# A transformer block on one core: query and key scratch doubled by parity, and the first layer norm's normal form made by GpSimd

## What is computed

```python
mod = (silu(c) @ wmod).reshape(16, 6, 1, 128)          # sa, ca, ga, sb, cb, gb per batch
h = layernorm(x) * (1 + ca) + sa                        # LN1
q, k, v = h @ wq.T + bq, h @ wk.T + bk, h @ wv.T + bv   # 16 heads of 8
scores = q @ k.T * 8 ** -0.5 + band                     # a key counts only within 32 tokens
x = x + ga * (softmax(scores) @ v @ wo.T + bo)
h = layernorm(x) * (1 + cb) + sb                        # LN2
top2 = top_k(softmax(h @ gate_w.T), 2)                  # 8 experts, 2 for each token
ffn = sum over the chosen e of (silu(s_e*h @ w1[e]) * (s_e*h @ w3[e])) @ w2[e]   # s_e: the score
x = x + gb * (ffn + the shared expert's silu(h @ w1s) * (h @ w3s) @ w2s)
```

## Time and profile before

| | us |
|---|---|
| median of three runs | 745.36 |
| the profiled execution | 746.85 |
| its span in the trace | 745.1 |

### The profile page before, as it was taken

How to read it: one execution, slowest core, us unless ns; L and a number is a source line. 1 busy time by engine, 2 the same in 40 slices (tenths; PEclk the granted TensorE clock), 3 DMA queues, 4 the chain that set the end, 5 groups by cost and what they waited for, 6 DMA issues and landing times.

```text
span 745.1 us, 18977 instructions
## 1 busy us (share of the span) xinstructions
PE 660.5 (89%) x5934; PEld 558.9 (75%) x5934; DVE 581.2 (78%) x1541; ACT 613.0 (82%) x2602; POOL 541.2 (73%) x564
## 2 busy tenths in 40 slices
PE   2267798999989999999899999989899989979886
PEld 1155677878878887878788887878788878878765
DVE  5446667988969898989889898969798888867553
ACT  4276779998979999999999899979899998875442
POOL 4430418887868989788878888868968886758784
PEclk9996557999989999999999999999999999999999
DMA  4747586777676777777677878577777676713120
GB/s 147 181 97 189 131 203 183 187 214 192 181 184 186 200 205 199 190 213 184 175 187 213 204 195 214 163 197 200 189 187 204 161 201 174 188 41 136 64 83 14
DMA packets 193860, 127.70 MB, mean 171 GB/s; under 512 B 110640, under 2 KB 170848, under 8 KB 193632
## 3 DMA queue, kind: packets, MB, share of 16 engines
q1 hardware_dynamic: 193760, 126.50, 64.3%
HBM read 96.29 MB, written 30.17 MB: 170 GB/s over the span
## 4 chain that ended last, share of the span: by engine, by line
PE 42%; DMA 22%; SPq 13%; POOL 8%; issue 6%; ACT 5%; DVE 3%; POOLq 0%; DVEq 0%; ACTq 0%
DMA k<-k_scr 15%; PE ps_s L1209 11%; PE ps_Y L1277 10%; SPq L315 8%; DMA r_scr<-rst 6%; PE ps_O L1232 5%; ACT p L675 4%; SPq L323 3%; PE ps_A L1152 3%; POOL xl L495 3%; POOL xs L489 2%; PE ps_M L1260 2%; PE ps_A L1153 2%; PE ps_A L1154 2%; PE ps_B L1152 2%
## 5 line engine op out<-in xcount | busy, mean ns | idle before, releaser
L675 ACT ACTIVATE p<-ps_s,nmx 128x96 f32<-128x96 f32 x1024 | 332.3, 345 | 58.4 <-DVE nmx L878 57.8
L675 ACT ACTIVATION_READ_ACCUMULATOR p<-ps_s,nmx 128x1 f32 x1024 | 215.7, 211 | 0.0
L1209 PE MATMUL ps_s<-k,q 128*128 128x96 f32 x1024 | 167.2, 297 | 54.1 <-DMA k<-k_scr 42.2
L1209 PEld LDWEIGHTS ps_s<-k,q 128*128 128x128 f32 x1024 | 147.6, 210 | 81.4 <-DMA k<-k_scr 50.2
L878 DVE TENSOR_REDUCE nmx<-ps_s 128x4 f32<-128x384 f32 x256 | 138.0, 548 | 67.4 <-PE ps_s L1209 64.0
L495 POOL TENSOR_TENSOR xl<-xs,xh 128x512 fp32r<-128x512 f32 x128 | 163.4, 1282 | 20.7 <-ACT xh L697 20.7
L489 POOL TENSOR_TENSOR xs<-h,sbc 128x512 f32<-128x512 f32 x128 | 164.0, 1287 | 4.1 <-DMA sbc<-s_scr 4.1
L1277 PE MATMUL ps_Y<-w2s,g 128*128 128x128 f32 x1152 | 163.4, 290 | 0.6 <-DVE g L984 0.6
L1277 PEld LDWEIGHTS ps_Y<-w2s,g 128*128 128x128 f32 x1152 | 150.2, 202 | 4.7 <-DVE g L984 0.8
L895 DVE STREAM_TRANSPOSE pt<-p 128x384 f32<-128x384 f32 x256 | 136.1, 558 | 6.1 <-PE ps_O L1232 4.4
L975 DVE SCALAR_TENSOR_TENSOR th<-th,ps_A 128x512 f32<-128x512 f32 x144 | 97.7, 678 | 36.2 <-ACT th L718 36.1
(11 more groups left out here) (119 smaller groups left out, 920.4 us busy)
## 6 DMA issues: line engine op xcount, KB each, us to landing
sbc<-s_scr SPq DMA_DIRECT2D x64, 512.0 KB, 5.6
k<-k_scr SPq DMA_DIRECT2D x64, 384.0 KB
q<-q_scr SPq DMA_DIRECT2D x128, 96.0 KB
k<-k_scr SPq DMA_DIRECT2D x32, 336.0 KB
q_scr<-qh SPq DMA_DIRECT2D x32, 256.0 KB, 2.5
k_scr<-kh SPq DMA_DIRECT2D x32, 256.0 KB, 2.6
xt<-x SPq DMA_DIRECT2D x16, 256.0 KB, 6.0
q_scr<-ql SPq DMA_DIRECT2D x16, 256.0 KB, 2.5
```

Source lines behind the costliest of these rows:

```text
L675: last = nc.scalar.activation(p[:, n % PRING, gg, :], ps_s[:, n % 2, MK * gg:MK * gg + MK], ACT.Exp, bias=nmx[:, n, gg:gg + 1], accum_out= ...
L1209: last = mm(ps_s[:, n % 2, MK * gg:MK * gg + MK], heads[:, h, gg, nl], k4[:, h, gg, :, MB * nl:MB * nl + MB], start=gg == 0, stop=gg == HG ...
```

## The change

Three things change.

- `q_scr` and `k_scr` get a leading dimension of 2. Batch b writes and reads the copy `b % 2`. The wait in `put_q(b)` on the loads becomes one on the loads of batch b-2, which are those of the same copy.
- The normal form of LN1 (`l1_xn`) is written by POOL, with four `tensor_scalar` instructions that multiply by the token's scale and add its shift. They stand right behind `shift`. ACT's `normal` stays for LN2 alone.
- `high_h1` waits for `q_mm` of the batch before as well, and `project_k` for `l1["hl"]`.

```diff
-        q_scr = nc.dram_tensor("q_scr", (HJ, 3, 32, S), F32, kind="Internal").ap()
-        k_scr = nc.dram_tensor("k_scr", (HJ, 3, 32, S), F32, kind="Internal").ap()
+        q_scr = nc.dram_tensor("q_scr", (2, HJ, 3, 32, S), F32, kind="Internal").ap()
+        k_scr = nc.dram_tensor("k_scr", (2, HJ, 3, 32, S), F32, kind="Internal").ap()
...
-            def put_q(b, loaded):
+            def put_q(b, par):
                 sp.wait_ge(q_h, b + 1)
-                if loaded is not None:
-                    sp.wait_ge(half_in[0], loaded)
-                    sp.wait_ge(half_in[1], loaded)
-                sp.dma_start(q_scr[:, 0].rearrange("j r s -> r j s"), qh[:].bitcast(F32)).then_inc(q_scr_w, 16)
+                if b >= 2:
+                    sp.wait_ge(half_in[0], 112 * (b - 1))
+                    sp.wait_ge(half_in[1], 112 * (b - 1))
+                sp.dma_start(q_scr[par, :, 0].rearrange("j r s -> r j s"), qh[:].bitcast(F32)).then_inc(q_scr_w, 16)
...
                 if has(b, -1, 1):
-                    put_q(b + 1, loaded)
-                    put_k(b + 1)
-                    load_half(b + 1, 0)
+                    put_q(b + 1, 1 - par)
+                    put_k(b + 1, 1 - par)
+                    load_half(b + 1, 0, 1 - par)
                     load_ga(b + 1)
...
+            def normal(b, s, ln, src):
+
+                pool.wait_ge(s["nm"], b + 1)
+                if not seq_is(b, 0):
+                    pool.wait_ge(s["tr"], b)
+                for a in range(NQB):
+                    nc.gpsimd.tensor_scalar(ln["xn"][:, a], src[:, a], ln["rstd"][:, a:a + 1], ln["nm"][:, a:a + 1],
+                                            ALU.mult, ALU.add).then_inc(s["xn"], 1)
...
                     shift(b + 1, l1, ln1)
+                    normal(b + 1, l1, ln1, xt)
...
                     act.wait_ge(v_mm, b)
+                    act.wait_ge(q_mm, b)
...
-                if has(b, -1, 1):
-                    normal(b + 1, l1, ln1, xt)
...
             def project_k(b):
 
+                pe.wait_ge(l1["hl"], b + 1)
```

More of the change, by code:

```diff
@@ L284, in load_gb, with put_k, load_half @@
                 sp.dma_start(grow[:], m_scr[bass.ds(b, 1), 1, :].to_broadcast([128, D])).then_inc(g_in, 16)
-            def put_q(b, loaded):
+            def put_q(b, par):
                 sp.wait_ge(q_h, b + 1)
-                if loaded is not None:
-                    sp.wait_ge(half_in[0], loaded)
-                    sp.wait_ge(half_in[1], loaded)
-                sp.dma_start(q_scr[:, 0].rearrange("j r s -> r j s"), qh[:].bitcast(F32)).then_inc(q_scr_w, 16)
-                sp.dma_start(q_scr[:, 2].rearrange("j r s -> r j s"), qh[:].bitcast(F32)).then_inc(q_scr_w, 16)
+                if b >= 2:
+                    sp.wait_ge(half_in[0], 112 * (b - 1))
+                    sp.wait_ge(half_in[1], 112 * (b - 1))
+                sp.dma_start(q_scr[par, :, 0].rearrange("j r s -> r j s"), qh[:].bitcast(F32)).then_inc(q_scr_w, 16)
+                sp.dma_start(q_scr[par, :, 2].rearrange("j r s -> r j s"), qh[:].bitcast(F32)).then_inc(q_scr_w, 16)
                 sp.wait_ge(q_l, b + 1)
-                sp.dma_start(q_scr[:, 1].rearrange("j r s -> r j s"), ql[:].bitcast(F32)).then_inc(q_scr_w, 16)
-            def put_k(b):
+                sp.dma_start(q_scr[par, :, 1].rearrange("j r s -> r j s"), ql[:].bitcast(F32)).then_inc(q_scr_w, 16)
+            def put_k(b, par):
                 sp.wait_ge(k_h, b + 1)
-                sp.dma_start(k_scr[:, 0].rearrange("j r s -> r j s"), kh[:].bitcast(F32)).then_inc(k_scr_w, 16)
-                sp.dma_start(k_scr[:, 1].rearrange("j r s -> r j s"), kh[:].bitcast(F32)).then_inc(k_scr_w, 16)
+                sp.dma_start(k_scr[par, :, 0].rearrange("j r s -> r j s"), kh[:].bitcast(F32)).then_inc(k_scr_w, 16)
+                sp.dma_start(k_scr[par, :, 1].rearrange("j r s -> r j s"), kh[:].bitcast(F32)).then_inc(k_scr_w, 16)
                 sp.wait_ge(k_l, b + 1)
-                sp.dma_start(k_scr[:, 2].rearrange("j r s -> r j s"), kl[:].bitcast(F32)).then_inc(k_scr_w, 16)
-            def load_half(b, h):
-                keys = k_scr.rearrange("j c (d g) s -> (j c d) g s", g=HG)
+                sp.dma_start(k_scr[par, :, 2].rearrange("j r s -> r j s"), kl[:].bitcast(F32)).then_inc(k_scr_w, 16)
+            def load_half(b, h, par):
+                keys = k_scr[par].rearrange("j c (d g) s -> (j c d) g s", g=HG)
                 if not seq_is(b, 0):
@@ L315, in load_half @@
                     sp.dma_start(q4[24 * j:24 * j + 24, h, :, :, j, :].bitcast(F32),
-                                 q_scr[j].rearrange("c (d g) (n q) -> (c d) g n q", g=HG, q=MB)
+                                 q_scr[par, j].rearrange("c (d g) (n q) -> (c d) g n q", g=HG, q=MB)
                                  [:, :, HB * h:HB * h + HB]).then_inc(half_in[h], 16)
@@ L362, in _ @@
             sp.dma_start(b_scr, mrow[:, 2]).then_inc(s_mw, 16)
-            put_q(0, None)
-            put_k(0)
+            put_q(0, 0)
+            put_k(0, 0)
             sp.wait_ge(s_mw, 32)
@@ L367, in _ @@
             sp.wait_ge(z_in[0], 1)
-            load_half(0, 0)
+            load_half(0, 0, 0)
             load_ga(0)
@@ L373, in _ @@
             sp.wait_ge(z_in[1], 1)
-            load_half(0, 1)
+            load_half(0, 1, 0)
             def body(b, par):
-                loaded = 112 * b + 112 if isinstance(b, int) else sp.snap(112 * b + 112)
                 if has(b, 1):
@@ L381, in body @@
                 if has(b, 0, 1):
-                    load_half(b, 1)
+                    load_half(b, 1, par)
                 if has(b, 2, 1):
@@ L544, in _ @@
             shift(0, l1, ln1)
+            normal(0, l1, ln1, xt)
             low_h1(0)
@@ L718, in expert @@
                 nc.scalar.activation(th[:, par], ps["A"][:], ACT.Tanh, scale=0.5).then_inc(th_d, 1)
-            normal(0, l1, ln1, xt)
             modulate(0, l1, h1[:], 0, "M1")
```

## The result

The change made the kernel faster by a little over half a per cent. In one comparison, 17 runs each, its median was 744.27 us and that of the kernel before 747.26 us; the ratio of the two kernels' times is put at 0.9944, with a 95% interval of 0.9918 to 0.997 (it isn't the quotient of the two medians, which is 0.996, nor that of the two means, 743.9 and 748.5, which is 0.994). The time itself lies 1.2 us from the predicted 745.5 and inside its range, but the forecast was "no difference" within 0.5%, and the ratio is 0.56% under 1, with an interval that leaves 1 out. The profiled execution of after took 748.45 us (span 746.7), the slowest of its 17 runs, while the one of before took 746.85.

The account below looks back on a forecast made before the run. Bound: PE's own stretch plus its wait at `scores(b, 8)` for half 1's transfer. Profiled 746.85 us, less 0.25 (body 0), plus 0.45 (body 2), gives 747.05; the profiled execution lay 1.49 above the median, so about 745.5; range 738.5 to 752.5.

Parts of the forecast that it names:

- no difference: Whole kernel: time within 0.5%, 3.7 us, of no change; chance 0.50.
- The bound: Steady bodies: a PE-bound stretch plus a transfer-bound one, PE idling 0.88 to 3.11 us at `scores(b, 8)`.
- The doubled scratch at 0: SP's 73.5 us of waits at L291 vanish, q writes leave 2.3 us earlier, gain 0.
- The announced signs: SP's waits in the profile after: L291 gone, L303 grown to some 4 us a body.
- Rival C: Earlier q writes delay half 1's landing: 752.5 us for half a write per body, 759 for a whole; chance 0.10.
- ACT without the normal form at 0: ACT loses 1.66 us a body but then waits for POOL's `xs` of expert 2: gain 0 in steady bodies.
- The price of the instruction: POOL's 128x128 tensor_scalar: 0.38 us taken, between 0.30 and 0.46; four cost 1.4 us (1.1 to 1.7).
- The delay that follows: POOL, so `hl` and PE before scores 8, 0.45 us late (0.1 to 0.8), still ahead of the landing.
- body 2: The only body without a wait of POOL for the router's reciprocal: +0.45 us, once.
- The clock, put at nothing in the sum: Rival A: POOL's lateness splits PE's idle time, five half-clock stretches after scores 8 go: 738.5 us; chance 0.27.
- The other objection: Against the clock rival: after a 3.11 us wait at scores 8 the clock stayed up for the first matmuls.
- the sign that the prediction named for A: Profile after: fewer or more than five stretches at half clock would make the forecast wrong.

Follow-up runs that it names:

- late kernels: The changed kernel, the change again, GpSimd only and idle work: four instructions in front of POOL's work, no filler; `hl` 14.60 to 14.72 us after `rst`.
- on-time ones: Six kernels: the one before, the control, scratch only, old wait, hidden, no normal form; `hl` 13.76 to 13.83 us after `rst`.
- the control: The kernel before, unchanged, run in the place of an experiment: ratio 1.001, mean 747.6 us.
- the change again: The changed kernel run once more, against the kernel before: ratio 0.9965, mean 743.8 us.
- dose series: The kernel before with no, four (ratio 0.9938) or eight (1.0119) idle tensor_scalar instructions on POOL behind the shift, and the filler.
- the filler: The kernel before with eight extra, unused matmuls on TensorE ahead of its wait at scores 8: ratio 0.979, again 0.985.
- scratch only: The kernel before with the doubled scratch and its waits; the normal form stays on ACT: ratio 0.9959.
- old wait: Scratch only, but `put_q` waits for the landings of the batch before, as in the kernel before: ratio 0.9959 against the kernel before.
- hidden: The kernel before with four idle tensor_scalar instructions on POOL ahead of the router's scores, where POOL waits anyway: ratio 0.9976.
- no normal form: The kernel before without LN1's normal form on any engine after the first batch: ratio 0.9962.
- GpSimd only: The kernel before with LN1's normal form moved to POOL and the two added waits, one scratch copy: ratio 0.9995.
- idle work: The kernel before with four idle tensor_scalar instructions on POOL behind LN1's shift; ACT keeps the normal form: ratio 0.9938.

## Why the prediction was right or wrong, point by point

**The bound: right.** PE's stretch and the transfer's stretch alternate, and scores 8 is where they meet. Moving the landing is worth 3%; taking 74 us of waits off SP is worth nothing that could be measured.

**The doubled scratch at 0: right as far as it can be measured.** The announced signs came: L291 gone, L303 grown, though to 2.6 us a time and not to 4. By two comparisons the doubled scratch is 0.4% faster, each with an interval that just takes in 1.00; by the means of all runs it is 0.2 and 0.1%. Its traces show no term that moved. Rival C didn't occur: the landings of after are where they were (12.29 against 12.33 us).

**ACT without the normal form at 0: right.** ACT waits for `xs` where it worked before, and leaving the work out altogether gained nothing that can be told from zero.

**The price of the instruction: within its bounds, off in the choice.** 449 ns, between 0.30 and 0.46, at the product's end and not at the 0.38 taken; four took 1.74 us and not 1.4 (1.1 to 1.7).

**The delay that follows: too small, and for one item of the queue worked out wrongly.** The prediction said that the 0.96 us that POOL waits for ACT "hides 0.96 of the 1.4", and left 0.45 (0.1 to 0.8). `hl` is late by 0.8 to 0.9 us on average in each kernel with the four instructions. The mis-sized duration is 0.3 of the difference and a gap of 0.1 us ahead of them the rest. The wait at scores 8 didn't cover all of it either: in the late kernels scores 8 starts 0.13 us behind the landing on average, against 0.04 in the on-time ones, 0.09 us a body. Worse, the wait hides nothing of what `xs` of expert 1 suffers, since that stands ahead of the wait. In body 2 there is no slack for it. ACT's rows of before and of after:

```profile
113.02 0.36 ACT L685 ACTIVATE rst<-ps_M 32x256 f32<-32x256 f32 x1
...
115.08 0.64 ACT L697 ACTIVATE xh<-xs 128x512 fp32r<-128x512 f32 x1
```

```profile
111.21 0.36 ACT L696 ACTIVATE rst<-ps_M 32x256 f32<-32x256 f32 x1
...
115.11 0.63 ACT L708 ACTIVATE xh<-xs 128x512 fp32r<-128x512 f32 x1 [1.73 <-POOL xs L497]
```

From the start of `rst` to this `xh` it was 2.06 us and is 3.90. The exponentials stand behind it on ACT, and TensorE waits for them at scores 5 of body 2, after and then before:

```profile
117.08 0.67 PE L1218 MATMUL ps_s<-k,q 128*128 128x96 f32 x2 [3.08 <-ACT p L686]
```

```profile
117.06 1.09 PE L1209 MATMUL ps_s<-k,q 128*128 128x96 f32 x4 [1.24 <-ACT p L675]
```

The extra is 1.84 us where the sum had 0.45. From scores 8 of body 1 to that of body 2 five of the six on-time traces took 37.7 to 37.8 us (the control 40.3, with a slower trip of the sums) and the four late ones 39.1 to 39.9. So this term was about four times too small. It points to a slower kernel, though, so it isn't what the forecast missed.

**The clock, put at nothing in the sum: the step that failed.** The prediction had it as rival A, with its place and its reason (POOL late, the idle time moved and split) and a chance of 0.27, and left it out of the sum, since "the idle time in sum is the same". The sum is the same indeed: the page gives 54.1 us of idle time before the matmuls of the scores in the kernel before and 54.0 in after. But it was the wrong measure: what counts is the length of one idle stretch. The other objection, that the clock stayed up after 3.11 us, holds only for the first matmuls: it was 1.00 from 490.8 to 492.6 us and 0.50 from 492.7 to 496.0. And the sign that the prediction named for A came: between 167 and 620 us the clock fell at five places in the kernel before, at three in after and at two in the change again. Over the 18 traces of the table, bodies 3 to 13, the waits at scores 8, and whether half clock followed before the next `rst`, stand like this:

| wait at scores 8, us | bodies | clock fell behind it |
|---|---|---|
| under 1.0 | 120 | 0 |
| 1.0 to 1.5 | 25 | 4 |
| 1.5 to 2.0 | 29 | 15 |
| 2.0 to 2.5 | 15 | 12 |
| over 2.5 | 9 | 7 |

Length alone doesn't decide: in the kernel before the clock fell after 1.66 us and stayed up after 1.96.

The on-time kernels waited 1.55 us a body and spent 1.79 us at half clock; the four late ones waited 0.93 and spent 0.78. By trace the half clock is 1.18 to 2.48 us in the six and 0.31 to 0.93 in the four, without overlap. The Trainium skill warns of this (TensorE: Matmul & The Clock Gate, section "Why this matters for your kernels"): idle gaps between bursts cost clock. The runs agree, and show it for gaps shorter than the page warns of; here the measurement decides. The PE part is shorter by 0.49 us a body (22.83 against 23.32), 5.4 us over bodies 3 to 13. Less 1.0 for scores 8 being late and 1.6 for body 2 that makes 2.8, beside the 3.5 measured. Behind `scores(14, 8)` nothing is gained (130.9 against 130.6 us). But the bodies' whole periods show only 0.23 us of it each (40.25 against 40.48). Some 0.1 of what is missing is the late scores 8; the other part of the period, with trips of the sums between 3 and 7 us, moves by as much from trace to trace. So that the clock is the mechanism rests on the dose series (none, four, eight, and the filler) and on the half clock by trace; its share in the 3.5 us is an estimate. It may be smaller than this: the four on-time variants (scratch only, old wait, hidden, no normal form), whose `hl` is on time, lie 1.4, 0.6, 4.3 and 2.2 us under the kernel before by the means of their own comparisons.

That the time lies 1.2 us from the predicted one is luck: the number was fixed on three runs of the kernel before with a median of 745.36 us, and all 115 average 747.4. This difference hides most of the gain.

What stays open: whether the scratch adds 1 us or nothing; why GpSimd only (746.0 +- 0.9) gained less than the change (743.9 +- 0.5) and the idle work (742.0 +- 1.2), with the same lateness, wait and half clock; why the on-time variants too lie a little under the kernel before, the hidden idle work (743.7 +- 1.4) the furthest; and what besides the length of a wait decides whether the clock falls.

## What to carry to other kernels

Where the busiest engine alternates between its own work and a wait for a transfer, look at the length of that wait as well as at its place: beyond its own length, such a wait can cost the clock of the stretch behind it. The lever is the transfer's chain (here 3% for four reads issued one wait earlier); failing that, something harmless for TensorE to do. And when work is put in front of a queue, price the delay for each item behind it on its own: slack further down the queue hides nothing for the item ahead of it.

## What the runs showed of the hardware that was not expected

- A GpSimd `tensor_scalar` of 128x128 fp32 with two operands per token takes 449 ns, nearly the 461 of a product of two tiles; reading one tile instead of two saved almost nothing.
- In body 1, where there is hardly any expert work, a half clock costs nothing. One trace had full clock there and the kernel before half clock; the stretch took 23.1 us in both. The windows, full clock first:

```profile
90.00:113.00 23.00, 21.16 (x183) 17.11 (x182) 14.71 (x53) 17.50 (x95) 6.74 (x12) 1.00 0.73 211
```

```profile
90.00:113.00 23.00, 21.09 (x182) 17.17 (x182) 13.99 (x52) 16.26 (x87) 6.93 (x11) 0.50 0.79 211
```

- The trip of the sums through DRAM, the same two small DMAs in every body, took between 2.7 and 7.6 us from the end of `rst` to the issue of its read, in the fifteen traces whose kernels issue nothing in between. That spread is more than the effect under test.
